# Layer 1's routing worked out from logits, with ranks made by TensorE and two-byte columns, and products that nothing reads in TensorE's waits

## The reference

```
logits = xf @ Wg                                    # (4096, 8)
probs = softmax(logits)
vals, idx = top_k(probs, 2)
w = vals / (sum(vals) + 1e-9)
for k in range(2):
    oh = one_hot(idx[:, k], 8)
    pos = cumsum(oh, axis=0) - 1 + counts           # rank of the token in its expert
    keep = (oh == 1) & (pos < 256)                  # at most 256 tokens for an expert
    counts += sum(keep)
    combine += w[:, k] * keep
for e in range(8):
    out += combine[:, e] * (gelu(xf @ W1[e] + b1[e]) @ W2[e] + b2[e])
x = x + gb * out
```

## Time and profile before

| | us |
|---|---|
| median of 3 runs (897.37 to 899.93) | 897.94 |
| the profiled execution | 897.85 |
| its span, first to last instruction | 895.6 |
| from the end of the logits to the fetch | 784.5 to 816.2 |
| from the fetch to the last products | 816.2 to 871.7 |
| from there to the end | 871.7 to 895.6 |

### The profile page before, as it was taken

How to read it: one execution, slowest core, us unless ns; L and a number is a source line. 1 busy time by engine, 2 the same in 40 slices (tenths; PEclk the granted TensorE clock), 3 DMA queues, 4 the chain that set the end, 5 groups by cost and what they waited for, 6 DMA issues and landing times.

```text
span 895.6 us, 33689 instructions
## 1 busy us (share of the span) xinstructions
PE 713.8 (80%) x14638; PEld 644.2 (72%) x14639; DVE 658.0 (73%) x1076; ACT 491.7 (55%) x724; POOL 558.3 (62%) x412
## 2 busy tenths in 40 slices
PE   4467636882688999999999999999999988915846
PEld 2137425771677999899989899988988887904846
DVE  3788553453587999999999999999998989284104
ACT  5465302342474677578668667757676656554310
POOL 4011046524257989988999988888878888404630
PEclk9677658996699999999999999999999999855978
DMA  7731142331006000000000000000000000420137
GB/s 192 242 79 48 49 90 58 71 64 54 21 5 193 6 10 7 6 7 10 7 6 10 18 4 4 15 4 3 4 15 4 4 15 16 149 100 26 46 105 200
DMA packets 67595, 44.01 MB, mean 49 GB/s; under 512 B 22000, under 2 KB 62208, under 8 KB 67328
## 3 DMA queue, kind: packets, MB, share of 16 engines
q1 hardware_dynamic: 64128, 35.11, 13.8%
q0 software_dynamic: 3328, 6.82, 3.3%
HBM read 27.76 MB, written 14.16 MB: 47 GB/s over the span
## 4 chain that ended last, share of the span: by engine, by line
PE 67%; DVE 10%; issue 9%; ACT 7%; another core or an unknown queue 3%; DMA 2%; SPq 2%; POOL 1%; DVEq 0%; POOLq 0%; ACTq 0%
PE psum L1811 16%; PE psum L1911 6%; PE psum L1866 6%; PE psum L1844 6%; PE psum L1902 4%; PE psum L1873 3%; PE psum L1859 3%; PE psum L1881 3%; PE psum L1745 2%; ACT arena L1007 2%; PE psum L2120 2%; PE psum L1760 2%; PE psum L1852 2%; PE psum L1620 1%
## 5 line engine op out<-in xcount | busy, mean ns | idle before, releaser
L1811 PE MATMUL psum<-hT,w_qkv 128*128 128x128 f32 x1408 | 173.9, 281 | 2.0 <-DVE arena L1363 1.6
L1811 PEld LDWEIGHTS psum<-hT,w_qkv 128*128 128x128 f32 x1408 | 164.5, 194 | 5.2 <-DVE arena L1363 1.8
L563 POOL TENSOR_TENSOR arena<-arena,small 128x1024 f32<-128x1024 f32 x56 | 106.0, 1914 | 56.1 <-DVE small L1376 56.1
L542 POOL TENSOR_TENSOR arena<-arena 128x1024 f32<-128x1024 f32 x56 | 106.7, 1905 | 12.6 <-ACT arena L890 11.4
L528 POOL TENSOR_TENSOR arena<-arena 128x1024 f32<-128x1024 f32 x56 | 106.5, 1902 | 0.0
L1369 DVE TENSOR_REDUCE small<-arena 128x16 f32<-128x1024 f32 x60 | 73.1, 1219 | 8.8 <-ACT arena L879 6.6
L518 POOL DMA_INDIRECT arena<-h_rows,route x40 | 40.2, 1004 | 58.1 <-issue 43.2
L567 POOL TENSOR_TENSOR arena<-arena 128x1024 f32<-128x1024 f32 x28 | 65.9, 2353 | 16.3 <-DVE arena L1396 16.2
L1357 DVE TENSOR_REDUCE small<-psum 128x16 f32<-128x1024 f32 x60 | 72.8, 1215 | 2.6 <-PE psum L1911 2.6
L1363 DVE TENSOR_TENSOR arena<-psum,small 128x1024 f32<-128x1024 f32 x60 | 70.5, 1215 | 0.1
L1844 PE MATMUL psum<-arena 64*128 64x64 f32 x1344 | 62.4, 231 | 10.0 <-issue 7.4
(11 more groups left out here) (319 smaller groups left out, 1643.7 us busy)
## 6 DMA issues: line engine op xcount, KB each, us to landing
y_rows<-hT SPq DMA_DIRECT2D x8, 512.0 KB, 6.6
arena<-y_rows SPq DMA_DIRECT2D x8, 512.0 KB, 6.0
o_rows<-arena SPq DMA_DIRECT2D x10, 256.0 KB
x_sb<-in_L_attn_u SPq DMA_DIRECT2D x8, 256.0 KB, 4.6
arena<-in_W_inT SPq DMA_DIRECT2D x16, 128.0 KB
arena<-in_W_out SPq DMA_DIRECT2D x64, 32.0 KB
h_rows<-arena SPq DMA_DIRECT2D x4, 512.0 KB, 3.3
h_rows<-hT SPq DMA_DIRECT2D x8, 256.0 KB, 2.3
```

Of the source, the lines that this page charges most:

```text
L542: pool.tensor_tensor(x3, x3, lr[:, tile_of(t) * 32 + k * H:tile_of(t) * 32 + k * H + H].unsqueeze(2).to_broadcast([P, H, D]), ALU.mult).th ...
L563: pool.tensor_tensor(z4, z4, r3.unsqueeze(3).to_broadcast([P, 8, 2, CH]), ALU.mult).then_inc(done, 1)
L1811: mm = pe.matmul(ps[bank][:, p * P:(p + 1) * P], w_qkv[:, j * HD + p * P:j * HD + (p + 1) * P], hT[:, at:at + P], start=True, stop=True)
```

## The change

The choice of experts is made from the logits less their maximum, without the softmax. The largest is where this is zero; the second is the largest after 1e30 is taken off at the first. The exponentials serve the weights alone: the first weight is 1 / (1 + exp(second) + 1e-9 * sum), the second that times exp(second). Tiles are counted chunk by chunk, (c, bp), and the first 24 tiles (chunks 0 to 5) are handled by `choose` before the logits of chunks 6 and 7 exist. The hot columns `oh1` are written as two-byte numbers with the tile innermost. `up_to` holds their running sums over chunks. TensorE adds up each token's rank in one accumulation group of matmuls over `oh1` and `up_to` with the masks, one of which (`first_half`) is new. `rhs1` has the layout (tile half, number, tile) in two-byte numbers throughout. Row numbers for the scatter are worked out behind the release of POOL. TensorE gets products of the identity by itself, which nothing reads: two at each of three places among the last logits, 18 before the slots, 46 behind them.

```diff
             act.wait_ge(oh_done, 2)
-            act.activation(pr1, sh1, ACT.Exp).then_inc(ex_done, 1)
+            act.activation(pr1, sh1, ACT.Exp)
+            act.activation(tile_f, tile_f, ACT.Exp).then_inc(ex_done, 1)
...
+            def choose(lg, c0, c1):
+                a, b = c0 * BP, c1 * BP
...
+                chain.link(dve.tensor_reduce(per(mx), part(lg), AX_X, ALU.max))
+                chain.link(dve.tensor_tensor(part(sh1), part(lg), wide(mx), ALU.subtract))
+                chain.link(dve.scalar_tensor_tensor(part(pick1), part(sh1), 0.0, order, ALU.is_equal, ALU.mult))
+                chain.link(dve.tensor_reduce(per(m2), part(pick1), AX_X, ALU.max))
+                chain.link(dve.tensor_tensor(hot(0), part(pick1), wide(m2), ALU.is_equal))
+                chain.link(dve.scalar_tensor_tensor(part(sh2), hot(0), -1e30, part(sh1), ALU.mult, ALU.add))
+                chain.link(dve.tensor_reduce(per(tile_f), part(sh2), AX_X, ALU.max))
+                chain.link(dve.tensor_tensor(part(sh2), part(sh2), wide(tile_f), ALU.is_equal))
+                chain.link(dve.tensor_tensor(part(sh2), part(sh2), order, ALU.mult))
+                chain.link(dve.tensor_reduce(per(m2), part(sh2), AX_X, ALU.max))
+                return dve.tensor_tensor(hot(1), part(sh2), wide(m2), ALU.is_equal)
...
+            dve.wait_ge(lg_mm, 2)
+            chain.link(choose(ps[1][:, L:L + T * E], 0, NC - 2))
+            for c in range(NC - 3):
+                chain.link(sum_up(c))
+            sum_up(NC - 3).then_inc(rhs_ready, 1)
+            dve.wait_ge(rhs_ready, 3)
+            dve.wait_ge(lg_mm, 3)
+            choose(ps[0][:, 0:T * E], NC - 2, NC).then_inc(oh_done, 1)
+            dve.wait_ge(oh_done, 2)
+            chain.link(sum_up(NC - 2))
+            sum_up(NC - 1).then_inc(rhs_ready, 1)
+            dve.tensor_tensor(et(numbers[:, 0:512]), et(oh1), over_e2(pair_no[:, :], E), ALU.mult)
+            chain.link(dve.tensor_scalar(numbers[:, 512:1024], oh1, part_no, None, ALU.mult))
...
+            dve.tensor_tensor(k3(scr1)[:, :, 0, :], k3(ranks)[:, :, 0, :], k3(oh1)[:, :, 0, :], ALU.mult)
+            chain.link(dve.tensor_scalar(cap1, total, float(CAP), None, ALU.min))
+            chain.link(dve.tensor_tensor(r3, k3(ranks)[:, :, 1, :], cap1.unsqueeze(2).to_broadcast([P, E, T]), ALU.add))
+            chain.link(dve.tensor_tensor(k3(scr1)[:, :, 1, :], r3, k3(oh1)[:, :, 1, :], ALU.mult))
+            chain.link(dve.tensor_reduce(pos, scr1.rearrange("p (e t) -> p t e", e=E), AX_X, ALU.add))
...
-            for c in range(3, NC):
+            for c in range(3, NC - 2):
                 second_turn(c)
                 second_logits(c - 2)
+            second_logits(NC - 4)
+            second_logits(NC - 3).then_inc(lg_mm, 1)
+            keep_warm(2, ps[0][:, L:L + P])
+            second_turn(NC - 2)
+            keep_warm(2, ps[0][:, L:L + P])
             second_logits(NC - 2)
+            keep_warm(2, ps[0][:, L:L + P])
+            second_turn(NC - 1)
             second_logits(NC - 1).then_inc(lg_mm, 1)
...
+            keep_warm(18, ps[2][:, 0:P])
             pe.wait_ge(f1_b, 64)
             turn_slots(0)
             slots_first(0)
...
             slots_second(E - 1)
+            keep_warm(46, ps[0][:, 0:P])
             pe.wait_ge(weights_made, 2 * BP)
```

More of the change, by code:

```diff
@@ L1508, in _ @@
[L1508 to L1514, removed]
-            dve.wait_ge(cnt_done, 2)
-            own, both, pref = ps[3][:, 512:1024], ps[2][:, 0:512], ps[3][:, 0:512]
@@ L1518, in _ @@
[L1518 to L1529, removed]
-            chain.link(dve.tensor_scalar(cnt1[:, 0:E], cnt1[:, 0:E], float(CAP), None, ALU.min))
-            chain.link(dve.tensor_tensor(o4[:, 1, :, :], o4[:, 1, :, :], cnt1[:, 0:E].unsqueeze(1).to_broadcast([P, BP, E]), ALU.add))
@@ L1532, in _ @@
-            r4, w4 = (ap.rearrange("p (k c e) -> p k c e", c=NC, e=E) for ap in (run1, own))
-            chain.link(dve.tensor_copy(r4[:, :, 0, :], k3(off1)))
-            for c in range(1, NC):
-                chain.link(dve.tensor_tensor(r4[:, :, c, :], r4[:, :, c - 1, :], w4[:, :, c - 1, :], ALU.add))
-            chain.link(dve.tensor_tensor(rk1, run1, pref, ALU.add))
-            chain.link(dve.tensor_tensor(scr1, rk1, oh1, ALU.mult))
-            chain.link(dve.tensor_reduce(pos, te(scr1), AX_X, ALU.add))
@@ L1540, in _ @@
-            second, row1, first = keep, e_of, scr1[:, 0:2 * T]
-            chain.link(dve.tensor_scalar(second, pos, float(P), None, ALU.is_ge))
-            chain.link(dve.scalar_tensor_tensor(row1, second, -float(P), pos, ALU.mult, ALU.add))
-            chain.link(dve.tensor_scalar(first, pos, float(P), None, ALU.is_lt))
-            chain.link(dve.scalar_tensor_tensor(second, pos, float(CAP), second, ALU.is_lt, ALU.mult))
-            r5 = numbers.rearrange("p (t m e) -> p t m e", m=2, e=E)
@@ L1548, in _ @@
[L1548 to L1552 removed]
+            chain.link(dve.scalar_tensor_tensor(row_f, e_sum, 1e-9, tile_f, ALU.mult, ALU.add))
+            chain.link(dve.tensor_scalar(row_f, row_f, 1.0, None, ALU.add))
@@ new lines, in _ @@
+            chain.link(dve.reciprocal(wk[:, 0:T], row_f))
+            dve.tensor_tensor(wk[:, T:2 * T], wk[:, 0:T], tile_f, ALU.mult).then_inc(wk_set, 1)
+            dve.wait_ge(cnt_done, 2)
+            ranks, total = ps[2][:, 0:512], ps[2][:, 512:512 + E]
+            k3 = lambda ap: ap.rearrange("p (e k t) -> p e k t", e=E, k=2)
+            r3 = rk1.rearrange("p (e t) -> p e t", e=E)
+            dve.tensor_tensor(k3(scr1)[:, :, 0, :], k3(ranks)[:, :, 0, :], k3(oh1)[:, :, 0, :], ALU.mult)
@@ L1556, in _ @@
             last.then_inc(rhs_ready, 1)
-            chain.link(dve.tensor_copy(rows_b[:, :], row1))
             for n in range(2 * T // 8):
```

119 lines of the change are left out of this document (65 added, 54 removed).

## The result

The changed kernel takes **895.1 us** (median of 20 executions, 888.3 to 900.1) where the kernel before takes 902.98 beside it (20 executions, 896.9 to 908.2): ratio **0.9902**, 95% interval 0.9878 to 0.9926. A ratio is worked out from the executions themselves and is not the quotient of the two medians, which can lie up to 0.005 away. On the median of 897.94 the ratio gives 889.1. The forecast was 883.8 (0.984). The gain is real and some 8 to 9 us, not 14. The profiled execution took 890.12 around a span of 888.4, 7.2 less than before.

What follows compares the result with a forecast made beforehand. The last part was taken as a series of stages, each waiting for the one before. Terms +3.5 - 13.2 - 0.9 - 1.5 - 2.0 = -14.1 took 897.9 to 883.8 us, range 878 to 889.

Steps and rivals of the forecast that it cites:

- Logits, +3.5: TensorE's last logits: reordered turns, copy waits and six dummy products at the lower clock end 3.5 us later, at 788.0.
- that rival (0.25): Dummies among the logits hold TensorE's clock, so the choice starts 3.7 us earlier: 880.1 us, or 878; chance 0.25.
- First part of the choice, 5.8 us and hidden: VectorE ranks tiles 0 to 23: 4.3 us of steps plus 1.5 of running sums, hidden behind the logits.
- Logits to first one-hot piece, 10.0: VectorE's routing from the logits' end to the first one-hot piece takes 10.0 us instead of 23.2: -13.2.
- Found numbers, 2.7 us from the last piece to the fetch: VectorE needs five steps instead of nine before releasing POOL's first fetch: 2.7 us instead of 3.6, -0.9.
- Slots, -1.5: 18 dummies before the slots warm TensorE, shortening the first product and POOL's wait: -1.5 us, bounds -2.9 and +1.9.
- comes about 2 earlier: Product two of slot 0 on TensorE, before at 828.3, comes about 2 us earlier after a first product of 1.9.
- Last products, -2.0: 46 dummies after slot 7 keep TensorE's clock up for the last products: -2.0 us, bounds -2.5 and +7.
- y_rows comes at 349 GB/s, 3.0 us a quarter: In the last products, y_rows is read at 349 GB/s, 3.0 us a quarter, faster than the warm products' 3.6.
- Zero: Constants at the start: about 0.7 us more POOL work, covered by its 3.7 us of idle, so no cost.
- does not come back for slots and last products: TensorE's clock stays at the lower level behind the dummies; only routing is saved, -10.6: 887.3 us; chance 0.15.
- Rival of 892: Dummies also stand before ready work, 20 us against 12.9, costing up to 5 more than 887.3: 892; chance 0.05.

Runs made afterwards that it cites:

- profile pair: First measurement of the changed kernel beside the kernel before, one profiled execution of each: 895.1 us against 902.98, ratio 0.9902.
- the pair again: Changed kernel and kernel before, both unchanged, measured and profiled again: changed 868.21 us, ratio 0.9919; the kernel before took 872.1 in one execution.

## Why the prediction was wrong

- **Logits, +3.5: nearly right (+4.1)** in the profile pair. The clock fell at 777, as taken, and the six did not hold it; that rival (0.25) is out. The waits for the copies were undersized: without the six, where both copies stand bare, the stage is 2.3 longer than in the old order, and two waits of the 0.75 taken would be 1.5. The six cost 1.9 and not 2.7.
- **First part of the choice, 5.8 us and hidden: 7.1 and hidden.** It misses the writes of two-byte columns at a stride, 1.02 us for 192 elements where 0.36 was taken, and 0.44 for 64 where 0.22.
- **Logits to first one-hot piece, 10.0: right (10.3).** The strided writes add 0.44 and the sum over 512 0.3 (1.02 us); the wait of 0.2 for the ranks did not come, and the small steps were a little shorter than taken. The two 1024 products took 1.29, as said.
- **Found numbers, 2.7 us from the last piece to the fetch: right.**
- **Slots, -1.5: failed, +0.6.** Products and first slot did as said (6.0 and 1.99 us). The failing step is that the second product of slot 0 "comes about 2 earlier" and POOL's wait shrinks with it. In the kernel before that wait was made mostly by a late release. In the changed one another release is late: VectorE takes the second turn 2.9 us after TensorE's end, "remote". So that product starts 13.3 us behind the first fetch instead of 12.1, and POOL waits 3.27 us instead of 2.87. The prediction said that it couldn't tell how that delay moves, and booked a gain all the same. Where releases were not late, in the pair again and in the kernel before with the 18 and 46, the term is -0.7 and -0.9. What makes releases late is open: it goes with the chip or the time of measuring and not with the change.
- **Last products, -2.0: failed, +2.0** (rows back +1.7, products +0.3). The failing step is "y_rows comes at 349 GB/s, 3.0 us a quarter": a rate read at the old address, and "Zero" for the constants at the start, which were costed on POOL alone. They shift the arena off a multiple of 256 bytes and the rate is 290. SP's second issue is also 1.1 us longer, which no term had. The gap that was forecast as 2.5 us is 3.56, and the clock goes. With the arena in place, last scatter to last product is 21.5 us in two executions, against 23.2 and 23.5 in the kernel before, so the term is -1.7 to -2.0; in a third, where the clock was lost, it is 23.0. Of the miss of 4.0 some 2 are the address's. The rival that the clock "does not come back for slots and last products" (887.3) was right on the last products, for the reason that it gave, the gap; in the slots the clock did come back (first product 1.99 us). Its time is the nearest to 889.1 in part by luck, since the slots and the read missed for reasons of their own.
- **Rival of 892.** 20 us against 12.9 are 7 more, and not "up to 5": 895. Nothing hangs on it, as the products ended before the rows came.

Sum of the profile pair: 4.1 - 13.9 + 0.6 + 1.7 + 0.3 = -7.2, against the forecast's -14.1; the misses are 2.1 in the slots, 4.0 behind them, 0.8 ahead of them. What the address does to the rate of the read is shown by exchange in both directions, and some 2 us of it in the stages; in the medians it is not shown. The long issue and the late releases are seen, not explained. Whether the products are worth anything in the median is open.

## What to carry to other kernels

A constant added ahead of a large buffer is a change of that buffer's address: look where each tile that a DMA writes starts before and after, and keep it at a multiple of 256 bytes. When two traces differ in a stage, go through every row of it before one cause is given the whole: here a second one stood in SP's timeline. When a clock or a wait is forecast to improve, ask what comes next in the chain, here the read of the rows, and whether its rate still holds. A product that nothing reads has to pay twice, in the stage and in the median; here the gain did not need it.

## What the runs showed of the hardware

- The same read of 4 MB in 512-byte rows goes at 346 to 349 GB/s into starts at multiples of 256 bytes and at 290 to 294 into the others.
- VectorE writing two-byte numbers at a stride of 128 bytes takes 871 ns for 160 elements, tile by tile (with strided reads instead) 442; float32 steps of 160 take 325. A sum over 512 whose 8 addends are 64 numbers apart takes 1.02 us.
- TensorE's clock was kept at 1.00 over 0.98 to 2.22 us of idle behind the 46 products in seven executions, one of them with an idle of 1.94; in an eighth it fell 0.8 us after an idle of 1.94, and in three it fell within 3.19, 3.39 and 3.56.
- SP's issue of a read of 512 KB takes 0.58 us as the second of the eight; in four executions it took 1.4 to 1.8 with an instruction fetch of 16 KB beside it, and the first quarter landed after 6.0 to 6.6 us instead of 5.4 to 5.6.
- The slots take 41.4 to 44.3 us on two chips and 47.6 to 49.9 on others, the same kernels and instructions. The traces of the others have waits that end by "remote" and those of the two have none; in the first pair such releases came some 3 us late, and POOL waits for their work.
